# Hybrid attention and expert block on one core: when TensorE multiplies the values of layer a

## The reference, cut to what matters

```
scores = einsum('bqhd,bkhd->bhqk', q, k) + einsum('bqr,bkr->bqk', q_rope, k_rope)[:, None]
scores = scores / scale
scores = where(causal, -inf, scores)
w      = softmax(scores, axis=-1)
attn   = einsum('bhqk,bkhd->bqhd', w, v)
x      = x + attn @ W_o
...
x = x + ffn(layernorm(x));  x = x + attn_b(layernorm(x));  x = x + ffn(layernorm(x))
```

## Time and profile before

| | before |
|---|---|
| median of 3 runs | 1052.27 us (1050.64 to 1055.45) |
| the profiled execution | 1052.97 us, of which the trace's span is 1051.3 us |
| PE (TensorE matmul) busy | 962.3 us, 92% |
| VectorE / ScalarE / GpSimd busy | 740.9 / 693.3 / 218.8 us |
| mean granted TensorE clock | 0.971 |
| attention of layer a | from about 60 to 331 us of the span |

### The profile page before, as it was taken

The page is one execution under the profiler, slowest core; times in us unless marked ns, Lnnn a source line. Parts: engine busy times, 40 slices in busy tenths (PEclk is TensorE's granted clock), DMA queues, the critical chain, the costliest instruction groups (busy, mean ns, idle before and its releaser), DMA issues. The chain is left out here.

```text
span 1051.3 us, 16044 instructions
## 1 busy us (share of the span) xinstructions
PE 962.3 (92%) x5694; PEld 625.3 (59%) x5694; DVE 740.9 (70%) x1310; ACT 693.3 (66%) x1188; POOL 218.8 (21%) x494
## 2 busy tenths in 40 slices
PE   3879999999998999999997799999999889999997
PEld 2545555665555777788774344444444366778886
DVE  4786667776732567789875967777777547678996
ACT  2426666666664689888835256666666669998885
POOL 1442355653332000000005112222232210000000
PEclk9989999999999699999999789999999999999999
DMA  3763443122112011245603370111000021114561
GB/s 90 213 156 60 134 122 88 35 75 78 61 41 81 0 41 41 70 125 153 123 14 104 81 188 22 32 32 32 2 1 2 2 80 41 41 60 125 145 145 50
DMA packets 67727, 78.52 MB, mean 75 GB/s; under 512 B 6512, under 2 KB 55552, under 8 KB 67264
## 3 DMA queue, kind: packets, MB, share of 16 engines
q1 hardware_dynamic: 62720, 73.62, 25.7%
q10 hardware_dynamic: 4928, 3.88, 1.4%
HBM read 53.44 MB, written 22.94 MB: 73 GB/s over the span
## 5 line engine op out<-in xcount | busy, mean ns | idle before, releaser
L1026 ACT ACTIVATE b_pt<-b_banks 128x512 f32<-128x512 f32 (+1 forms) x320 | 154.9, 559 | 100.4 <-PE b_banks L946 99.9
L1301 PE MATMUL f_banks<-f_xr,f_w1r 128*128 128x512 f32 x768 | 191.3, 397 | 0.6 <-ACT f_h L1386 0.6
L1317 PE MATMUL f_banks<-f_hr,f_w2r 128*128 128x512 f32 x768 | 189.1, 394 | 3.1 <-DVE f_hr L1412 2.5
L1386 ACT ACTIVATE f_h<-f_banks,b_t 128x512 f32<-128x512 f32 x256 | 167.1, 682 | 31.8 <-PE f_banks L1301 29.3
L1412 DVE TENSOR_TENSOR f_hr<-f_h,f_hr 128x1024 fp32r<-128x1024 f32 x128 | 156.2, 1223 | 28.4 <-ACT f_hr L1392 26.5
L1301 PEld LDWEIGHTS f_banks<-f_xr,f_w1r 128*128 128x128 f32 x768 | 143.2, 191 | 29.6 <-ACT f_h L1386 1.5
L1317 PEld LDWEIGHTS f_banks<-f_hr,f_w2r 128*128 128x128 f32 x768 | 141.7, 188 | 31.7 <-issue 3.4
L1045 DVE TENSOR_REDUCE a_mlate<-a_banks 128x2 f32<-128x1024 f32 (+3 forms) x120 | 125.0, 1080 | 49.1 <-PE a_banks L901 30.9
L1045 DVE TENSOR_REDUCE b_mlate<-b_banks 128x2 f32<-128x1024 f32 (+3 forms) x120 | 125.8, 1080 | 36.3 <-PE b_banks L911 18.2
L1392 ACT ACTIVATE f_hr<-f_h 128x1024 fp32r<-128x1024 f32 x128 | 136.0, 1062 | 4.1
L1026 ACT ACTIVATE a_q_hl<-a_banks 128x512 f32<-128x512 f32 (+1 forms) x160 | 81.3, 557 | 73.7 <-PE a_banks L946 72.1
(11 more groups left out here) (196 smaller groups left out, 1054.7 us busy)
## 6 DMA issues: line engine op xcount, KB each, us to landing
scratch_w<-a_tab SPq DMA_DIRECT2D x16, 512.0 KB, 3.1
f_w1r<-scratch_w SPq DMA_DIRECT2D x16, 512.0 KB, 4.7
f_w2r<-scratch_w SPq DMA_DIRECT2D x16, 512.0 KB, 5.4
v<-scratch_gate SPq DMA_DIRECT2D x32, 256.0 KB, 5.4
xt<-scratch_gate SPq DMA_DIRECT2D x32, 256.0 KB, 5.0
a_rot<-in_w SPq DMA_DIRECT2D x16, 256.0 KB, 3.8
scratch_q<-a_q_hl SPq DMA_DIRECT2D x24, 128.0 KB, 2.8
a_q<-scratch_q SPq DMA_DIRECT2D x8, 384.0 KB
```

The lines of the kernel that those rows point to most:

```text
L1026: act.activation(pt[at % NPT][:, h, 0:cols], st[u % NST][:, 0:cols], ACT.Exp, scale=scale).then_inc(exp_done, 1)
L1301: last = pe.matmul(h_ps[:, j, :], w1r[e % 2][:, wp, j * P:(j + 1) * P], xr[xp][:, chunk(c)], start=(i == 0), stop=(i == 2))
L1317: last = pe.matmul(y_ps[:, q % 2, :], w2r[e % 2][:, wp, j * P:(j + 1) * P], hr[q % 2][hp][:, j, :], start=(j == 0 and i == 0), stop=(j == ...
L1386: act.activation(h[q % 2][:, j, :], h_ps[:, j, :], ACT.Gelu, bias=m.b1_t[:, e * HB + j:e * HB + j + 1]).then_inc(gelu_done, 1)
```

## The change

`BURST` for layer a is rewritten, and a new table `REST` takes over the sets that are left of the half before. Layer a now has four bursts per group:

- late half: after set 0 all three sets of the early half before; after set 2 sets 0 and 1; after set 5 sets 2, 3 and 4
- early half: after set 0 the last two sets (5 and 6) of the late half, and nothing more

At the very end the last early half's three sets come after its scores. Layer b's two tables are written in the new form too, and give the same order as before. In the whole program that makes 32 bursts of layer a in place of 48. The matmuls are the same. The programs of VectorE, ScalarE, GpSimd and SyncE keep every row and its place.

```diff
-BURST = {"a": [[(-2, -1), (0,), ()], [(-2, -1), (0,), (), (1, 2), (), (3, 4), ()]],
-         "b": [[(-2,), (-1,), (0,)], [(-2,), (-1,), (0,), (1,), (2,), (3,), (4,)]]}
+BURST = {"a": [[(), (), ()], [(), (), (0, 1), (), (), (2, 3, 4), ()]],
+         "b": [[(), (), (0,)], [(), (), (0,), (1,), (2,), (3,), (4,)]]}
+REST = {"a": [(0, 1, 2), (5, 6)], "b": [(1, 2), (5, 6)]}
...
                 if v % GH == GH - 1:
+                    if i:
+                        rest = REST[kind][HALVES[i - 1][1]]
+                        for s in rest if latent and v < GH else rest[v // GH:v // GH + 1] if not latent else ():
+                            values(i - 1, s)
                     for s in BURST[kind][c][v // GH]:
-                        if s < 0 and i:
-                            values(i - 1, s + len(SETS[HALVES[i - 1][1]]))
-                        elif s >= 0:
-                            values(i, s)
-        for s in (-2, -1):
-            values(NH2 - 1, s + len(SETS[HALVES[NH2 - 1][1]]))
+                        values(i, s)
+        for s in REST[kind][HALVES[NH2 - 1][1]]:
+            values(NH2 - 1, s)
         turn_o(NH2 - 1)
```

## The result

The changed kernel takes 1059.95 us in the median of 20 runs (1054.4 to 1064.37) against 1053.5 (1044.9 to 1058.65) for the one before beside it: ratio 1.0064, interval 1.0043 to 1.0084. That is 6.7 us slower (4.5 to 8.9).

A forecast was written before the change was run, and what follows sets the result against it. Layer a goes at TensorE's pace, with waits for maxima and the two-slot ring. Five steady groups +5.1, first group +0.3 and last +0.4 give +5.8 us on 1052.27: 1058.1 us, 8-in-10 range 1051.5 to 1062.

The forecast's parts named there:

- The late half's first score waits for its maxima: Layer a, early half: the score starts when its maxima's DMAs land, so removing 1.17 us of work ahead gains nothing.
- rival 1: Late half's first score isn't held by its maxima, so saved switches reach the end: 1046.4 us, chance 0.10.
- What a burst costs: TensorE in layer a: 0.86 us per set plus a fixed 0.37 per burst; sixteen bursts fewer make 5.9 us less work.
- The late half: Layer a: -0.70 us up to the last burst, where ring waits return part of the saving, then +0.86 for three sets.
- The steady group: Layer a: 0.86 - 0.70 + 0.86 = +1.02 us per group, five such +5.1 us.
- The last group: Layer a's end, without pieces, ScalarE pacing TensorE: +0.4 us, bounds -0.5 and +1.0.
- The first group: Layer a up to the first full period: +0.3 us, bounds -0.6 and +1.0.
- rival 4: New idle time in layer a's groups lowers the clock: 3.4 us per group, about 1080 us, chance 0.03.
- rival 2: Late half: the maxima hold but the ring doesn't; 0.38 us per group, 1054.3 us, chance 0.17.
- rival 3: Bursts of three starve ScalarE or VectorE; 8 groups by 0.43, 3.5 us more, 1061.6 us, chance 0.12.

The follow-up runs named there:

- early-half run: Changed kernel with the late half's three bursts of before put back, so only the early half differs from before: ratio 1.0064 against the kernel before, period 33.88 us.
- seven-burst run: Kernel before, with the late half's burst of sets 1 and 2 split into two bursts: period 33.35 us, +0.33.
- late half only: Changed kernel with the early half's burst of set 0 put back, late half's joined bursts kept: ratio 0.9987 against the kernel before, period 33.18 us.

## Why the prediction was right

**The late half's first score waits for its maxima.** Right: 3.55 us behind the start of its DMAs, forecast 3.54, and 1.17 us of work gone for nothing. The early-half run isolates it (+0.87 for one set's 0.86), and sending half of the DMAs over a second queue moves the score. The piece ahead of it came as walked too: 0.3 of the 1.17 was to be left, and it comes 4.87 us behind the burst (172.07 - 167.20) instead of 5.19, 0.32 sooner. What I didn't draw from my own walk is that the ring alone would keep most of the gain with no maxima in the way; rival 1 lets all of it through as soon as the DMAs land early enough. The runs with `turn_m` sooner show otherwise: even then only 0.41 of 1.07 gets through. The ring is a second lock behind the first.

**What a burst costs.** A set 0.86, right. The fixed price was taken as 0.37 from 0.33 to 0.40; the seven-burst run measures 0.33, the lower end, in one place. The Trainium skill's rule (TensorEngine Tiling (Array Packing), Key Properties: changing the mode drains the engine) is borne out as a price, and the result bears out that it isn't one that a removal pays back: rival 1, which took the 16 prices off the time, fails. What decides is who is waited for next.

**The late half.** Forecast -0.70 + 0.86 = +0.16, measured +0.17 alone. The walk holds piece by piece, counted from the end of the rest's burst: the piece ahead of `turn_o` was to come after 175.32 - 171.79 = 3.53 us and came after 181.49 - 177.97 = 3.52; `turn_o` after 4.82, came after 4.92; the next piece after 5.97, came after 5.96. The wait of `turn_o` was forecast as 0.8 and is 0.77.

**The steady group.** +1.02 forecast, +1.04 measured; five such are 5.2 us. No clock below 1.00 stands in them: from 84.20 to 353.90 us it is 1.00.

**The last group.** +0.4 forecast; from the burst of sets 5 and 6 to the final `turn_o` it takes 340.02 - 301.98 = 38.04 us, before 330.06 - 292.52 = 37.54: +0.5. The parts fit as well: from the rest's burst to the last burst of sets 5 and 6 it takes 0.71 us more (forecast +0.75), from there to the end 0.21 less (forecast -0.35).

**The first group: the term that was mis-sized.** I took +0.3 and bounded it by +1.0. Steady groups and the end make 5.2 + 0.5 = 5.7 us of 6.7, which leaves 1.0 with an interval of some 2 us on either side, so the total alone can't tell. The profile can: from the first score of the first late half to the first full period it takes 131.70 - 80.36 = 51.34 us, before 127.45 - 78.39 = 49.06. That is +2.3, outside my bounds, though the total came within 1 us of the forecast. The first score of the first group's late half now waits for its DMAs for 1.68 us, where PE waited 0.49 before (its weight load 0.69), and right behind it the granted clock is 0.50 for 3.4 us, in the row at 80.80 above. TensorE is busy all through that row, so by estimate half of it, 1.7 us, is lost. That leaves 0.6 for what the +0.3 stood for. The kernel with `turn_o` behind unit 14, whose clock stayed at 1.00 there, agrees: 126.42 - 76.92 = 49.50, +0.4. So rival 4, which I ruled out for the steady groups rightly, does happen, in one place, and I had looked only at idle times up to 0.7 us. The last section says how often.

**The total.** Forecast +5.8 us (1058.1), measured +6.7 (1059.95, beside 1053.5 for the kernel before). How near the total comes owes something to chance: by these parts an execution in which the clock falls in the first group is 5.2 + 2.3 + 0.5 = 8.0 us longer, one in which it doesn't 6.3, and no run here counts how many of the 20 did.

**Rivals 2 and 3.** A period of 33.4 would have been rival 2, one above 34.4 rival 3. With 34.06 both fall: the ring's waits are there, and the bursts of three starve nobody; ScalarE has 21.23 us of work in a group of 34.1.

## What to carry to other kernels

Before saving a fixed cost on the busiest engine, find the next instruction on it that waits for something else, and ask whether what it waits for moves too; here the maxima's DMAs hung on work ahead of the saved burst, and beside them stood a ring of two slots. Work taken out ahead of such a point becomes idle time, and if it is put back behind the point, it is paid a second time. Look for a limit that no list of waits names (here the distance from a DMA to its reader, equal in two places), and then move its producer sooner. Moving `turn_m` did that and took waits of the ring away as well; the two together were worth 1.1% with six bursts (0.9893) and 1.6% with four (0.9906 against 1.0064). Sending the maxima sooner alone was worth 0.45 of these 2.18 us per group.

## What the runs showed of the hardware

- **A longer wait went with a fall of the clock, though not every time.** With set 0's burst out of the early half and `turn_m` in its old place, the first group's first score waits 1.68 or 1.69 us for its DMAs. In three of the four profiles of such kernels (the change, the early half only, the maxima sent sooner) the granted clock fell from 1.00 to 0.50 within 1 us of the score's start and stayed there for 3.4 us; in the fourth (`turn_o` later) it stayed at 1.00. In the three profiles where the same wait is 0.49 us (before, late half only, seven bursts) it stayed at 1.00 too, and the waits of up to 0.77 in the steady groups never changed it. Nor did a wait of 1.64 us before the first score of layer a (60.61 us, kernel before): the clock stayed at 1.00 until 65.6. The Trainium skill says that an idle array falls back to half clock (TensorE: Matmul & The Clock Gate, Part 1); these traces agree, and show that the same wait in the same kernel family may or may not do it. What decides is not shown.
- **The low clock at the start of layer a varies by itself.** Between 60 and 75 us the granted clock is 0.77 before and 0.54 after, with the same order of work up to there. That is 13.8 us at the low level against 6.9 (0.46 and 0.23 of 15 us, by a half), and in the kernel with `turn_o` behind unit 14 there is none. In the profile after, the DMAs of the first late half's maxima start at 76.83 instead of 74.87, behind work that the change doesn't move; so 2.0 of the 4.25 us by which the first period begins later (131.70 against 127.45) are not the change's. Other kernels with the change's early half and `turn_m` in its old place begin theirs at 126.42 to 129.45. It is also why whole times of one execution each say nothing about an edit of this size.
- **A short item in a ring of two slots can hold TensorE up.** `turn_m` needs VectorE for 0.27 us, but a piece behind it waited 0.46 for the reduction of the item before. With it moved by one piece, a stretch in which nothing waited for its result became 0.88 us shorter.
